# Row statistics taken in the stage before, turns interleaved with router weights, root ahead of weight copies

## Chip, cores and metric

The kernel runs on one core of a Trainium2 chip. The metric is the device time of one execution in microseconds; the median of the runs is compared. The engines are TensorE (PE), VectorE (DVE), ScalarE (ACT), GpSimd (POOL) and SyncE (SP, which only issues transfers here).

## The reference

Two transformer-like layers on x of 2048 tokens by 256 features, all float32. Each of six sublayers normalizes x first:

```python
def _layernorm(x, axis=-1, eps=1e-05):
    m = jnp.mean(x, axis=axis, keepdims=True)
    v = jnp.var(x, axis=axis, keepdims=True)
    return (x - m) / jnp.sqrt(v + eps)
...
    x = x + 0.5 * _L0_ffn_ref(_layernorm(x), ...)   # routed: 64 of 512 tokens by weight W_r, gelu FFN
    x = x + _L0_attn_ref(_layernorm(x), ...)        # latent attention, 16 heads, causal
    x = x + 0.5 * _L0_ffn_ref(_layernorm(x), ...)   # the same routed FFN
    x = x + 0.5 * _L1_ffn_ref(_layernorm(x), ...)   # sum over 8 factors, 256 x 256
    x = x + _L1_attn_ref(_layernorm(x), ...)        # attention, 16 heads of 16, rotary, causal
    x = x + 0.5 * _L1_ffn_ref(_layernorm(x), ...)
```

The change touches how mean and variance of each token are taken and when, and the order of the work that follows a normalization. Nothing else of the computation changes.

## The kernel before

x stays in SBUF all the time as 16 tiles (NT) of 128 tokens by 256 features; four tiles make a chunk (NCH = 4, CH = 512 tokens). The stages follow each other with a barrier of all engines between them (`core.end_step`): ffn_a (routed), the projections of the latent attention (latp, norm latn) and its heads (lath), ffn_b (routed), mix_a (factors), the projections of the second attention (attp, norm attn), its heads (atth), its output (atto), and mix_b, which also stores the result. Every engine has one instruction queue and works it in order; instructions wait on semaphores.

A stage with a normalization begins with `Norm.statistics` on DVE: for each of the 16 tiles `bn_stats` (L238), then for each `bn_aggr` (L241) to mean and variance, then variance + eps (L243). ACT takes the root (L259; a table load for Sqrt stands ahead of it when another function's table is in place), DVE makes 1/root with one correction step (L270 to L274). `Norm.scale` (L249) then writes the normalized tiles xn, one instruction per tile. `Turn` transposes xn: PE makes eight transposes per chunk (L204) into two PSUM banks, DVE copies one (L188), ACT the other (L193).

- **Routed stages.** `norm.vector` scales all tiles and copies all of DVE's banks before w_r_wide, the router weights spread over 128 columns, is written (L345). PE turns all four chunks, then multiplies w_r_wide with each chunk (L437); ACT copies the rows of weights (L414), PE transposes them (L443), DVE picks them up (L352) and compares all tokens with all (L358, 16 instructions, 128 x 2048 to bf16). In ffn_b SP also loads the eight factors of the mix stages; POOL waits for them and for all of xn, adds them up (L335, seven instructions) and halves the bias (L337).
- **mix stages.** Turns and products with the summed factors (L550) are already interleaved. DVE adds each result of two tiles to x (L521, eight pairs); POOL adds the bias to x (L512).
- **lath.** A planner writes the order of each engine out by hand. At its end, DVE: fold (L1320), reciprocal of the sums (L1326), scaling (L1333) and the additions to x, two tiles each (L1339), in the chunk order 0, 3, 2, 1 for each pair of heads.
- **attp.** SP loads Wq, Wk, Wv, Wo (L1579), then rotary tables and a select matrix. POOL fills v_one with ones (L1628), a single instruction of 128 x 4608. PE waits for the weights, transposes them (L1693), then runs `norm.tensor`. ACT copies the four turned weights (L1644), then select (L1646), and only then takes the root and its share of the turns. DVE runs `norm.vector`. The first projection product is L1704.
- **atto.** Turns of the attended values, products (L1985), additions of pairs to x on DVE (L1968).

Of the kernel before, what the change touches and what calls it, by code (L numbers as in the profile page):

```python
# [13 lines left out]
P = 128  # L14
# [76 lines left out]
class Core:  # L91


    def __init__(self, nc, ctx, inp):
# [6 lines left out]
        self.half_bias = self.sb("half_bias", [P, DIM], F32)  # L101
        self.ident = self.square[:, 0, :]
# [65 lines left out]
class Turn:  # L168
# [21 lines left out]
    def scalar(self, act):  # L190
        for b in range(1, 2 * NCH, 2):
            act.wait_ge(self.turned, b + 1)
            self.core.nc.scalar.activation(self.place(b), self.banks[b % len(self.banks)][:], ACT.Copy).then_inc(self.evac_act, 1)  # L193
# [19 lines left out]

class Norm:
# [5 lines left out]
    def __init__(self, core, ctx, tag, xn, xn_t, banks, loading=None):  # L220
        self.core, self.xn, self.loading = core, xn, loading
        self.stats = core.sb(f"{tag}_stats", [P, NT, 6], F32, ctx)
        self.moments = core.sb(f"{tag}_moments", [P, NT, 2], F32, ctx)
# [9 lines left out]
    def statistics(self, dve, link):  # L233
        nc, x = self.core.nc, self.core.x
        for t in range(NT):
            if self.loading and t % TPC == 0:
                dve.wait_ge(self.loading.x_loaded[t // TPC], 16)
            s = nc.vector.bn_stats(self.stats[:, t, :], x[:, t, :])  # L238
        link(s)
        for t in range(NT):  # L240
            s = nc.vector.bn_aggr(self.moments[:, t, :], self.stats[:, t, :])  # L241
        link(s)
# [8 lines left out]

    def vector(self, dve, link):
# [4 lines left out]
    def scalar(self, act):  # L257
        act.wait_ge(self.var_ready, 1)
        self.core.nc.scalar.activation(self.root[:], self.var[:], ACT.Sqrt).then_inc(self.root_ready, 1)  # L259
        self.turn.scalar(act)  # L260
# [16 lines left out]
def routed_ffn_stage(core, tag, first=False):  # L277
# [3 lines left out]
    with ExitStack() as ctx:  # L281
# [20 lines left out]
        norm = Norm(core, ctx, tag, xn, xn_t, bank, loading)  # L302
# [6 lines left out]
        with nc.Block() as block:  # L309
# [31 lines left out]
            def _(dve):  # L341
                link = Link(core, dve, f"{tag}_dve_link")
                norm.vector(dve, link)
                dve.wait_ge(s["weights_loaded"], 32)
                nc.vector.tensor_copy(w_r_wide[:], w_r[:].unsqueeze(2).broadcast_to([P, ND, P])).then_inc(s["wide_ready"], 1)  # L345
                if first:
# [3 lines left out]
                for c in range(NCH):  # L350
                    dve.wait_ge(s["weight_turned"], c + 1)
                    w = nc.vector.tensor_copy(weight[:, TPC * c:TPC * (c + 1)],  # L352
                                              bank[4 + c][:].rearrange("p (t q) -> p t q", q=P)[:, :, 0])
# [52 lines left out]
            def _(act):  # L406
                if first:
                    loading.scalar(act)
                norm.scalar(act)

                act.wait_ge(s["weights_loaded"], 32)
                for c in range(NCH):
                    act.wait_ge(s["weight_bank"], c + 1)
                    nc.scalar.activation(weight_row[:, c * CH:(c + 1) * CH], bank[c][:], ACT.Identity,  # L414
# [1606 lines left out]
```

## Time and profile before

| | us |
|---|---|
| runs of the kernel | 1922.64, 1924.5, 1932.9 (median 1924.5) |
| profiled execution, its own time | 1925.92 |
| its span in the trace | 1924.2 |
| PE busy | 1711.6 (89%) |
| DVE busy | 1513.2 (79%) |
| ACT busy | 1181.4 (61%) |
| POOL busy | 1004.6 (52%) |

The busy shares are means over stages with different limits. The long stages (lath from about 160 to 1215, atth from about 1420 to 1870) keep PE busy; the short ones between them have stretches in which a single engine works. Line numbers are those of the kernel before. A matmul in float32 is two instructions in the trace where its moving side is wide, and the trace's granted clock is 1.00 for 2.4 GHz and 0.50 for 1.2 GHz.

### The profile page before, as it was taken

To read this page: it belongs to the slowest core of one execution; us is meant where nothing else is said; L and a number is where in the kernel's file an instruction comes from. 1 tells how busy PE (TensorE), PEld (TensorE's weight loads), DVE (VectorE), ACT (ScalarE), POOL (GpSimd) and SP (SyncE) were. 2 spreads that over 40 slices of the span, in tenths; PEclk is the share of its full clock that TensorE was granted. 3 is DMA by queue.
4 is the path that set the end of the run, shared out by engine and by line. 5 is a ranking of instruction groups with operands and counts; after the bars stand their busy time and mean duration, and the time that the engine had idled before them with its cause. 6 is when DMAs were issued, how large, how long until landed. Compare 5 with 4: busy or idle time off the path is not lost. (4 is left out here: it accounts for less than half of the span.)

```text
span 1924.2 us, 27185 instructions
## 1 busy us (share of the span) xinstructions
PE 1711.6 (89%) x9368; PEld 996.5 (52%) x9368; DVE 1513.2 (79%) x2231; ACT 1181.4 (61%) x2043; POOL 1004.6 (52%) x829
## 2 busy tenths in 40 slices
PE   4667999999999999999999999566979899999986
PEld 3544555556565555565565554365644344444445
DVE  6772888998897988998879898576566988888815
ACT  1045787787776777777777776201325377778760
POOL 0004799897896997988979978202412000000111
PEclk8786999999999999999999999777977699999998
DMA  3100000000000000000000000301440200110001
GB/s 102 59 21 24 1 1 1 15 1 8 8 1 15 1 1 15 1 13 3 1 7 1 1 1 1 94 1 39 77 78 2 34 2 2 22 15 2 2 1 44
DMA packets 26697, 34.34 MB, mean 18 GB/s; under 512 B 5312, under 2 KB 19648, under 8 KB 26432
## 3 DMA queue, kind: packets, MB, share of 16 engines
q1 hardware_dynamic: 25360, 31.28, 6.8%
q8 instruction: 76, 1.25, 0.3%
q10 hardware_dynamic: 1200, 1.31, 0.2%
q14 instruction: 61, 0.50, 0.1%
HBM read 26.03 MB, written 6.29 MB: 17 GB/s over the span
## 5 line engine op out<-in xcount | busy, mean ns | idle before, releaser
L1225 POOL TENSOR_TENSOR lath_summed<-lath_summed,lath_held 128x512 f32<-128x512 f32 x392 | 525.0, 1339 | 54.4 <-ACT lath_held L1131 27.5
L1942 ACT ACTIVATE atth_probs<-atth_score 128x512 f32<-128x512 f32 (+3 forms) x640 | 293.1, 538 | 141.4 <-PE atth_score L1861 139.8
L1296 DVE TENSOR_TENSOR lath_held<-lath_held,lath_shift 128x1024 f32<-128x1024 f32 (+2 forms) x352 | 331.2, 968 | 24.6 <-PE lath_shift L1044 15.1
L1125 ACT ACTIVATE lath_held<-lath_score 128x1024 f32<-128x1024 f32 (+2 forms) x352 | 283.8, 829 | 104.9 <-DVE lath_largest L1249 51.5
L1131 ACT ACTIVATE lath_held<-lath_held 128x1024 f32<-128x1024 f32 (+2 forms) x352 | 292.6, 861 | 48.8 <-DVE lath_held L1296 47.2
L1901 DVE TENSOR_REDUCE atth_maxima<-atth_slot 128x2 f32<-128x1024 f32 (+3 forms) x288 | 287.1, 1042 | 42.2 <-PE atth_slot L1844 41.3
L1031 PE MATMUL lath_out<-lath_held,lat_latent 128*64 128x512 f32 (+1 forms) x1152 | 302.9, 590 | 8.0 <-ACT lath_held L1131 4.4
L1015 PE MATMUL lath_score<-lath_query_hi,lat_key_hi 128*128 128x512 f32 x576 | 246.7, 428 | 22.9 <-ACT lath_held L1125 17.7
L1789 POOL TENSOR_SCALAR_AFFINE_SELECT atth_probs<-atth_probs 128x512 f32<-128x512 f32 x64 | 40.7, 636 | 419.4 <-ACT atth_probs L1942 419.4
L1020 PE MATMUL lath_score<-lath_query_hi,lat_key_lo 128*128 128x512 f32 x576 | 231.1, 401 | 0.0
L1249 DVE TENSOR_TENSOR lath_largest<-lath_score,lath_largest 128x1024 f32<-128x1024 f32 (+2 forms) x240 | 211.6, 882 | 17.6 <-PE lath_score L1020 12.6
L1016 PE MATMUL lath_score<-lath_query_lo,lat_key_hi 128*128 128x512 f32 x576 | 219.6, 381 | 0.0
L1015 PEld LDWEIGHTS lath_score<-lath_query_hi,lat_key_hi 128*128 128x128 f32 x576 | 108.8, 189 | 155.0 <-issue 80.6
L1231 POOL TENSOR_TENSOR lath_turn_a<-lath_query,lat_rope 128x512 f32<-128x512 f32 x64 | 86.5, 1352 | 189.9 <-DVE lath_turn_b L1302 155.3
L1874 PE MATMUL atth_out<-atth_probs,att_v_one 128*32 128x512 f32 (+3 forms) x1280 | 151.2, 553 | 0.5 <-POOL atth_probs L1789 0.5
L1020 PEld LDWEIGHTS lath_score<-lath_query_hi,lat_key_lo 128*128 128x128 f32 x576 | 110.3, 192 | 19.9
L1016 PEld LDWEIGHTS lath_score<-lath_query_lo,lat_key_hi 128*128 128x128 f32 x576 | 109.2, 190 | 14.5
L1861 PE MATMUL atth_score<-atth_query,att_key 50*128 50x512 f32 (+3 forms) x384 | 114.3, 440 | 2.8 <-ACT atth_probs L1942 2.6
L1031 PEld LDWEIGHTS lath_out<-lath_held,lat_latent 128*64 128x64 f32 x1152 | 61.8, 135 | 92.4 <-issue 69.6
L1302 DVE TENSOR_TENSOR lath_turn_b<-lath_turn_b,lat_rope 64x512 f32<-64x512 f32 x64 | 76.6, 1198 | 31.2 <-ACT lath_turn_b L1158 29.7
L1861 PEld LDWEIGHTS atth_score<-atth_query,att_key 50*128 50x128 f32 x384 | 51.8, 186 | 90.9 <-ACT atth_probs L1942 82.9
L1241 POOL TENSOR_TENSOR lath_query_lo<-lath_query,lath_query_hi 128x512 fp32r<-128x512 f32 x64 | 83.8, 1310 | 15.1 <-ACT lath_query_hi L1165 15.1
(345 smaller groups left out, 2889.2 us busy)
## 6 DMA issues: line engine op xcount, KB each, us to landing
att_first_query<-att_scratch SPq DMA_DIRECT2D x12, 256.0 KB, 9.1
atth_query<-att_scratch SPq DMA_DIRECT2D x12, 256.0 KB, 9.8
ffn_a_w<-in_L_ffn_W SPq DMA_DIRECT2D x2, 1024.0 KB
lat_raw_out<-in_L_attn_w_out SPq DMA_DIRECT2D x8, 256.0 KB, 2.7
lat_rope<-in_c_rope_feature SPq DMA_DIRECT2D x1, 2048.0 KB, 10.3
ffn_b_w<-in_L_ffn_W SPq DMA_DIRECT2D x2, 1024.0 KB, 7.1
ffn_b_factors<-in_L_ffn_factors SPq DMA_DIRECT2D x8, 256.0 KB, 5.0
att_scratch<-attp_high SPq DMA_DIRECT2D x4, 512.0 KB, 3.2
```

Of the source, the lines that this page charges most:

```text
L1015: nc.tensor.matmul(scores, key_hi[:, keys], hi, start=True, stop=False)
L1016: nc.tensor.matmul(scores, key_hi[:, keys], lo, start=False, stop=False)
L1020: last = nc.tensor.matmul(scores, key_lo[:, keys], hi, start=False, stop=True)
L1031: last = nc.tensor.matmul(by_head(out_bank[KL * i:KL * i + KL, :], q0), latent[:, kt, 0:KL], by_head(slot(n)[:, i, :], q0), start=(step == ...
L1125: nc.scalar.activation(part_columns(slot(n), tiles, q0), part_columns(score_bank[n % 2], tiles, q0), ACT.Copy)\
L1131: nc.scalar.activation(columns, columns, ACT.Exp, scale=SCALE0)\
L1225: nc.gpsimd.tensor_tensor(total, total, slot(n)[:, i, :], ALU.add).then_inc(s["tiles_summed"], 1)
L1249: nc.vector.tensor_tensor(out, first, second, ALU.max).then_inc(s["maxed"], 1)
L1296: nc.vector.tensor_tensor(columns, columns, added, ALU.subtract)\
L1861: nc.tensor.matmul(score_bank[u % 3][:, q0:CH], key_rows(GROUP * g + h, PLACED + 2, kt * P, P), query_rows(n, h, PLACED + 2, q0, CH - q0), ...
L1901: nc.vector.reduce_max(maxima[:, n % 2, :, pair, i, at], slot[r % 2][:, :, begin:begin + width], AX.X)\
L1942: nc.scalar.activation(probs[:, step % PROB_STEPS, h, q0:CH], score_bank[u % 3][:, q0:CH], ACT.Exp, scale=SCALE1)\
```

## The change

1. A class `Measure` takes `bn_stats` of tiles as soon as x is final in them and `bn_aggr` a little later, both on DVE, in the stage that finishes x: in lath for ffn_b, in mix_a for attn, in atto for mix_b. `Norm(..., measured=True)` then skips both loops; the other three norms (ffn_a, latn, mix_a) keep them. The places for them, row_stats and row_moments, are now shared.
2. At the end of ACT's work in lath and in atto stands a Sqrt of one column.
3. In both routed stages DVE scales two chunks, writes w_r_wide, then alternates copies of turned banks with the scaling of the next chunk; PE alternates turns and router products; ACT alternates its turn copies with the copies of the weight rows. Turns use banks 0 to 3, products 4 to 7, the transposed rows 0 to 3.
4. In attp ACT takes the root first and two turn copies before the weight copies, PE turns two chunks before it waits for the weights, and DVE alternates scaling and copies.

```diff
+class Measure:
+    def count(self, tiles):
+        for t in tiles:
+            self.core.nc.vector.bn_stats(self.core.row_stats[:, t, :], self.core.x[:, t, :]).then_inc(self.counted, 1)
...
+    def gather(self, dve, tiles):
+        dve.wait_ge(self.counted, max(self.count_of[t] for t in tiles))
+        for t in tiles:
+            self.core.nc.vector.bn_aggr(self.core.row_moments[:, t, :], self.core.row_stats[:, t, :]).then_inc(self.gathered, 1)
...
     def statistics(self, dve, link):
+        if not self.measured:
...
+    def scale_and_turn(self, dve):
+        self.scale((0, 1))
+        for c in range(2, NCH):
+            self.turn.vector(dve, (c - 2,))
+            self.scale((c,))
+        self.turn.vector(dve, range(NCH - 2, NCH))
```

The routed stages, on DVE, ACT and PE:

```diff
-                norm.vector(dve, link)
+                norm.statistics(dve, link)
+                norm.scale((0, 1))
                 dve.wait_ge(s["weights_loaded"], 32)
                 nc.vector.tensor_copy(w_r_wide[:], ...).then_inc(s["wide_ready"], 1)
+                for c in range(2, NCH):
+                    norm.turn.vector(dve, (c - 2,))
+                    norm.scale((c,))
+                norm.turn.vector(dve, range(NCH - 2, NCH))
...
-                norm.scalar(act)
-
+                norm.take_root(act)
                 act.wait_ge(s["weights_loaded"], 32)
...
+                norm.turn.scalar(act, (0, 1))
+                for c in range(2, NCH):
+                    take_row(c - 2)
+                    norm.turn.scalar(act, (c,))
+                for c in range(NCH - 2, NCH):
+                    take_row(c)
...
+                norm.turn.tensor(pe, (0, 1))
+                pe.wait_ge(s["wide_ready"], 1)
+                for c in range(2, NCH):
+                    weigh(c - 2)
+                    norm.turn.tensor(pe, (c,))
+                for c in range(NCH - 2, NCH):
+                    weigh(c)
```

mix_a (atto has the same four lines after its addition, and both end with a last gather and a wait for all):

```diff
+                        if measure:
+                            dve.wait_ge(added, b + 1)
+                            measure.count((2 * b, 2 * b + 1))
+                            if b:
+                                measure.gather(dve, (2 * b - 2, 2 * b - 1))
```

lath, on DVE (`last_chunk` is the last of the 32 chunks of all head pairs), and at the end of ACT's queue:

```diff
                     if kind == "fold": ...
+                        if n == 2 * last_chunk + 1:
+                            measure.count(tiles_of(last_chunk - 1))
                     elif kind == "turn_sums_out": ...
+                        if n == last_chunk:
+                            measure.gather(dve, [t for k in range(last_chunk - 3, last_chunk) for t in tiles_of(k)])
                     elif kind == "project_out": ...
+                        if n == last_chunk - 1 and part:
+                            wait_projected(n, part)
+                            measure.count(tiles_of(n - 2) + tiles_of(n - 1))
+                        elif n == last_chunk:
+                            wait_projected(n, part)
+                            measure.count(tiles_of(n, (part,)))
+                measure.gather(dve, tiles_of(last_chunk))
+                measure.wait_all(dve)
...
+                nc.scalar.activation(core.table_scratch[:], core.ones[:, 0:1], ACT.Sqrt)
```

attp, on DVE, ACT and PE:

```diff
-                norm.vector(dve, Link(core, dve, "attp_link"))
+                norm.statistics(dve, Link(core, dve, "attp_link"))
+                norm.scale_and_turn(dve)
...
+                norm.take_root(act)
+                norm.turn.scalar(act, (0, 1))
                 for m in range(4):
                     act.wait_ge(s["weights_turned"], m + 1)
...
+                norm.turn.scalar(act, range(2, NCH))
                 act.wait_ge(s["select_loaded"], 32)
...
-                norm.scalar(act)
...
+                norm.turn.tensor(pe, (0, 1))
                 pe.wait_ge(s["weights_loaded"], 64)
...
-                norm.tensor(pe)
+                norm.turn.tensor(pe, range(2, NCH))
```

## Rows read from the trace of the kernel before

**Rows 1.** The page's first part: busy time, share of the span, instructions of each engine.

```profile
PE 1711.6 (89%) x9368; PEld 996.5 (52%) x9368; DVE 1513.2 (79%) x2231; ACT 1181.4 (61%) x2043; POOL 1004.6 (52%) x829
```

**Rows 2.** Timeline, start of ffn_b: start us, us, engine, line, operation, count, idle before.

```profile
1216.25 1.28 ACT L259 ACT_TABLE_LOAD   x1 [7.33 <-PEq L122]
1216.29 5.33 DVE L238 BATCH_NORM_STATS2 ffn_b_stats<-x 128x6 f32<-128x256 f32 x16 [0.91 <-PEq L122]
...
1222.85 0.17 DVE L243 TENSOR_SCALAR ffn_b_var<-ffn_b_moments 128x16 f32<-128x16 f32 x1
...
1224.43 5.25 DVE L249 TENSOR_SCALAR ffn_b_xn<-x,ffn_b_moments,ffn_b_rstd 128x256 f32<-128x256 f32 x16
```

**Rows 3.** Timeline, PE in the turns and router products of ffn_a, then ffn_b.

```profile
17.96 6.23 PE L204 MATMUL ffn_a_bank<-square,ffn_a_xn 128*128 128x128 f32 x32 [17.96 <-DVE ffn_a_xn L249]
...
24.73 7.13 PE L437 MATMUL ffn_a_bank<-ffn_a_xn_t,ffn_a_w_r_wide 128*128 128x512 f32 x16 [0.55 <-DVE ffn_a_w_r_wide L345]
...
1225.86 6.44 PE L204 MATMUL ffn_b_bank<-square,ffn_b_xn 128*128 128x128 f32 x32 [11.21 <-DVE ffn_b_xn L249]
```

**Rows 4.** Timeline, DVE at the end of the heads stage lath.

```profile
1204.42 0.85 DVE L1320 TENSOR_TENSOR lath_out_whole<-lath_out,lath_half 64x256 f32<-64x256 f32 x2 [3.33 <-ACT lath_half L1144]
...
1214.69 0.69 DVE L1339 TENSOR_TENSOR x<-lath_side,x 128x512 f32<-128x512 f32 x1 [0.93 <-PE lath_side L1070]
```

**Rows 5.** Timeline of ffn_b's compares, POOL beside them; by line: ns min/median/max.

```profile
1233.23 1.29 POOL L335 TENSOR_TENSOR mixed<-ffn_b_factors 128x512 f32<-128x512 f32 x1 [27.99 <-DMA ffn_b_factors<-in_L_ffn_factors]
...
1241.97 1.71 DVE L358 TENSOR_SCALAR ffn_b_not_above<-ffn_b_weight_row,ffn_b_weight 128x2048 bf16<-128x2048 f32 x1
...
1242.64 2.62 POOL L337 TENSOR_SCALAR half_bias<-half_bias 128x256 f32<-128x256 f32 x1
...
1243.60 1.41 DVE L358 TENSOR_SCALAR ffn_b_not_above<-ffn_b_weight_row,ffn_b_weight 128x2048 bf16<-128x2048 f32 x1
...
L358 DVE TENSOR_SCALAR ffn_b_not_above<-ffn_b_weight_row,ffn_b_weight x16: 1268/1273/1711, 1242.0 to 1260.6; 128x2048 bf16<-128x2048 f32 x16
...
L1302 DVE TENSOR_TENSOR lath_turn_b<-lath_turn_b,lat_rope x64: 687/1212/1829, 155.1 to 1125.0; 64x512 f32<-64x512 f32 x64
```

**Rows 6.** Timeline, end of mix_a and start of attp.

```profile
1318.17 1.28 DVE L521 SCALAR_TENSOR_TENSOR x<-mix_a_bank,x 128x512 f32<-128x512 f32 x2
...
1324.91 0.69 DVE L521 SCALAR_TENSOR_TENSOR x<-mix_a_bank,x 128x512 f32<-128x512 f32 x1 [0.96 <-PE mix_a_bank L550]
1326.56 3.94 POOL L1628 MEMSET att_v_one<- 128x4608 f32 x1 [7.33 <-POOLq L122]
1326.60 5.33 DVE L238 BATCH_NORM_STATS2 attn_stats<-x 128x6 f32<-128x256 f32 x16 [0.99 <-PEq L122]
...
1332.41 3.68 PE L1693 MATMUL attp_bank<-square,attp_raw 128*128 128x128 f32 x16 [7.54 <-DMA attp_raw<-in_L_attn_Wo]
...
1337.81 0.25 DVE L270 RECIPROCAL attn_rstd<-attn_root 128x16 f32<-128x16 f32 x1 [4.47 <-ACT attn_root L259]
...
1340.37 3.67 PE L204 MATMUL attp_bank<-square,att_attended 128*128 128x128 f32 x16 [4.28 <-DVE att_attended L249]
...
1344.93 1.94 PE L204 MATMUL attp_bank<-square,att_attended 128*128 128x128 f32 x16 [0.89 <-DVE attp_xn_t L188]
...
1346.71 1.88 PE L1704 MATMUL attp_bank<-attp_w_qkv_t,attp_xn_t 128*128 128x512 f32 x4
```

**Rows 7.** Timeline, end of atto and start of mix_b.

```profile
1889.23 0.69 DVE L1968 TENSOR_TENSOR x<-atto_bank,x 128x512 f32<-128x512 f32 x1 [1.03 <-PE atto_bank L1985]
...
1890.88 5.32 DVE L238 BATCH_NORM_STATS2 mix_b_stats<-x 128x6 f32<-128x256 f32 x16 [0.96 <-PEq L122]
...
1897.43 0.17 DVE L243 TENSOR_SCALAR mix_b_var<-mix_b_moments 128x16 f32<-128x16 f32 x1
```

**Rows 8.** Busy time by stretch in the attention heads; PEclk is the granted clock.

```profile
1440.00:1460.00 20.00, 20.00 (x103) 10.31 (x103) 9.01 (x18) 9.09 (x22) 3.18 (x5) 0.50 0.01 2
1464.00:1484.00 20.00, 19.88 (x173) 10.36 (x175) 16.28 (x25) 14.46 (x42) 5.72 (x9) 1.00 0.01 2
```

More of the change, by code:

```diff
@@ L188, in vector, with scalar @@
             self.core.nc.vector.tensor_copy(self.place(b), self.banks[b % len(self.banks)][:]).then_inc(self.evac_dve, 1)
-    def scalar(self, act):
-        for b in range(1, 2 * NCH, 2):
+    def scalar(self, act, chunks=range(NCH)):
+        for b in (ND * c + 1 for c in chunks):
             act.wait_ge(self.turned, b + 1)
@@ L234, in statistics @@
         nc, x = self.core.nc, self.core.x
[L235 to L242, printed above, removed]
+        if not self.measured:
+            for t in range(NT):
+                if self.loading and t % TPC == 0:
+                    dve.wait_ge(self.loading.x_loaded[t // TPC], 16)
+                s = nc.vector.bn_stats(self.stats[:, t, :], x[:, t, :])
+            link(s)
+            for t in range(NT):
+                s = nc.vector.bn_aggr(self.moments[:, t, :], self.stats[:, t, :])
+            link(s)
         nc.vector.tensor_scalar(self.var[:], self.moments[:, :, 1], LN_EPS, None, ALU.add).then_inc(self.var_ready, 1)
@@ L301, in routed_ffn_stage @@
         loading = Loading(core, ctx) if first else None
-        norm = Norm(core, ctx, tag, xn, xn_t, bank, loading)
+        norm = Norm(core, ctx, tag, xn, xn_t, bank[:4], loading, measured=not first)
         names = ("weights_loaded ffn_loaded wide_ready weight_bank row_ready weight_turned compared counted chosen_ready"
@@ L431, in _, with weigh @@
             def _(pe):
-                norm.tensor(pe)
-                pe.wait_ge(s["wide_ready"], 1)
-                for c in range(NCH):
+                def weigh(c):
                     norm.turn.wait_chunk(pe, c)
                     for k in range(ND):
-                        last = nc.tensor.matmul(bank[c][:], w_r_wide[:, k, :], xn_t[:, k, c * CH:(c + 1) * CH],
+                        last = nc.tensor.matmul(bank[4 + c][:], w_r_wide[:, k, :], xn_t[:, k, c * CH:(c + 1) * CH],
                                                 start=(k == 0), stop=(k == ND - 1))
                     last.then_inc(s["weight_bank"], 1)
+                if first:
+                    pe.wait_ge(loading.square_loaded, 16)
+                norm.turn.tensor(pe, (0, 1))
[5 more added lines that the diff above has]
+                    weigh(c)
                 for c in range(NCH):
@@ L442, in _ @@
                     for i in range(TPC):
-                        last = nc.tensor.transpose(bank[4 + c][:, i * P:(i + 1) * P],
+                        last = nc.tensor.transpose(bank[c][:, i * P:(i + 1) * P],
                                                    weight_row[:, c * CH + i * P:c * CH + (i + 1) * P], core.ident)
@@ L503, in mixed_ffn_stage @@
         bank = [ctx.enter_context(nc.psum_tensor(f"{tag}_bank{i}", [P, CH], F32)) for i in range(8)]
-        norm = Norm(core, ctx, tag, xn, xn_t, bank[:4])
+        norm = Norm(core, ctx, tag, xn, xn_t, bank[:4], measured=out is not None)
+        measure = Measure(core, tag) if out is None else None
         mixed_done, added, biased, stored = (core.sem(f"{tag}_{n}") for n in ("mixed_done", "added", "biased", "stored"))
@@ L963, in latent_heads @@
         side_free = [core.sem(f"lath_side_free{i}") for i in range(2)]
+        measure = Measure(core, "lath")
+        last_chunk = NCH * PAIRS - 1
         def side(event):
@@ L1255, in _, with tiles_of, wait_projected @@
                 dve.wait_ge(s["vector_constants"], 1)
+                def tiles_of(k, parts=range(2)):
+                    return [TPC * LATENT_CHUNKS[k % NCH] + 2 * part + i for part in parts for i in range(2)]
+                def wait_projected(k, part):
+                    dve.wait_ge(freed(("project", k, part)), use["project", k, part] // 2 + 1)
                 for kind, n, *a in plan["vector"]:
@@ L1960, in attention_output @@
         projected, added = core.sem("atto_projected"), core.sem("atto_added")
+        measure = Measure(core, "atto")
         with nc.Block() as block:
@@ L1973, in _ @@
                 turn.scalar(act)
+                nc.scalar.activation(core.table_scratch[:], core.ones[:, 0:1], ACT.Sqrt)
             @block.tensor
```

42 lines of the change are left out of this document (31 added, 11 removed).

## The prediction

> **What bounds the kernel now.** I read the busy shares first [rows 1]: TensorE (PE) is busy for 89% of the span, VectorE (DVE) for 79%, so over the whole kernel the change can matter only where PE stands idle. Then the timeline at each stage start. There the picture is the same in ffn_b, attn and mix_b: all engines met at a barrier, PE has nothing to do, and one chain on DVE runs alone: 16 statistics of 256 columns (5.33 us), 16 aggregates (1.2 until the variance), variance, root, reciprocal, then the scaling of which PE needs four tiles before its first turn. In ffn_b the first DVE instruction is at 1216.29, the variance at 1222.85, scaling at 1224.43, PE at 1225.86 [rows 2, 3]. These microseconds are on the path one for one. The prices I use: 0.33 us per statistic and 0.07 per aggregate back to back (5.33/16, 1.2/16), and about 0.04 for a wait on an own semaphore. Third come the ends of the stages before, where the statistics go: what is idle there on DVE [rows 4, 6, 7].
>
> **The change part by part**, S being DVE's first instruction of a stage in the trace, S' the same after the change.
>
> *ffn_b, statistics out.* The variance comes at S instead of S + 6.56 (1222.85 - 1216.29): **-6.56**. The table load of 1.28 that hid behind the statistics [rows 2] moves to the end of the heads stage, where ScalarE (ACT) is idle; cost 0, and 1.1 if it stayed.
>
> *Heads stage, statistics in.* Twelve of sixteen tiles are counted in DVE's gaps: eight (2.7 us) after the last but one chunk's addition, ahead of an instruction before which DVE idled 3.33, four (1.4) and twelve aggregates (0.9) in later gaps [rows 4]; 0, for nobody is queued behind them on DVE before those gaps end. Of the last chunk two tiles fit into the 0.93 idle before the last addition (needed: 0.04 + 0.74). What follows that addition is bare: wait 0.04, two statistics 0.74, wait, four aggregates 0.4: **+1.2**.
>
> *Turns interleaved with router weights (ffn_a and ffn_b).* Before, PE ran 32 transposes (6.23 and 6.44), waited 0.55 for w_r_wide, then 7.13 of router products [rows 3]: 13.9 from first to last. The transposes took about 0.2 each, twice the 0.11 of the fast stretch of attn [rows 6], so this was TensorE at 1.2 GHz. After, PE has the same work without the wait: 32 x 0.11 + 6.9 = 10.4 us at 2.4 GHz, plus half of the time until the clock rises. If it rises 5 to 5.6 us after PE starts, as the pace of [rows 3] says, that is 12.9 to 13.2, a gain of 0.7 to 1.0; if after 3.7, as in attn [rows 6], 1.6. DVE keeps up: two chunks 2.6, wide copy 0.3, copy 0.7, then 1.3 per chunk. ACT's row copies stand behind turns in one queue, but each waits for products that PE issues earlier. **-1.0 each, -2.0.** DVE now waits for the weights at about S' + 4.3 with the scaling of chunks 2 and 3 queued behind, and PE behind that. The trace has no such wait; in attn a megabyte had landed 5.8 after the stage's start [rows 6], and here the two loads are tiny and issued first: 0, at most 1.5.
>
> *What the earlier compares meet.* The 16 compares of ffn_b come about 8 us earlier against GpSimd (POOL), whose seven additions of factors wait for a DMA and don't move (S + 17, [rows 5]). Before, only the last addition and the half_bias scaling overlapped them: the first compare took 1.71 instead of 1.27, the next 1.41, so DVE lost 0.44 + 0.14 + 0.14 = 0.7. After, compares begin near S' + 18 with some five or six additions left. Cheapest, as half_bias: twice 0.14 each, 1.6 in all. Dearest, as the slowest DVE product beside POOL in the heads (1829 against 687, 1.14 each [rows 5]): 6 x 1.14 = 6.8 more. Below nothing too: if compares kept POOL out altogether, -0.7. An addition reads twice half_bias's columns from two inputs, so I take a middle price of 0.7 each: **+3.5**, ends -0.7 and +7.
>
> The Trainium skill, "SBUF — State Buffer", section "Who interferes with whom", says that a VectorE instruction in a two-port mode (tensor_scalar from SBUF to SBUF can be one) and a GpSimd instruction lock each other out for the whole instruction. By that rule the first compare's 0.44 is right, but half_bias, 2.62 long while two compares each lost only 0.14, is not plainly so. It speaks against this change in two places; what it gives is rival B.
>
> *mix_a, statistics in.* After each pair's addition DVE now waits (0.04), counts two tiles (0.66) and aggregates two older ones (0.14): 0.69 + 0.84 = 1.53 per pair, against the 1.65 in which PE delivers one (0.69 and 0.96 idle, [rows 6]). But DVE starts late: the first two pairs fit ahead of the copy that precedes 1318.17; from there six pairs come back to back, 1318.2 + 6 x 1.53 = 1327.4, and a last wait with aggregates 0.3. Before it ended at 1325.60. **+2.1** (bounds 1.1, the bare tail alone, to 2.5). PE isn't held: it needs the addition four pairs back.
>
> *attn.* Before: DVE's variance was ready early, but the root stood behind the weight copies in ACT's queue (DVE idle 4.47), PE turned at S + 13.8, and the first projection product came at 1346.71, S + 20.1 [rows 6]. After: root at once, scaling possible at S' + 1.6. There POOL's memset of v_one runs until S' + 3.9. Statistics ran beside it undisturbed (5.33, as in ffn_b), but the scaling is of the compares' kind, which POOL delayed [rows 5]; no row shows one beside a memset. Bounds: 0 and 2.3; I take 2.3 as the compare is the nearer row. Then scaling at S' + 3.9, PE 1.43 later at 5.35 with 48 transposes (16 turns, 16 weight turns whose data landed at 5.8, 16 turns): 3.7 us at 1.2 GHz do 17 of them, 31 x 0.11 the rest, so the product at about **S' + 12.6**: **-7.5**. Without the memset's delay it would be about 10.2. The ACT queue moves too: two turn copies, four weight copies, two turn copies, select; select is first needed only after the first products, and the DMA that it waits for is issued as before: 0.
>
> *atto and mix_b.* Pairs of atto come every 1.72 (0.69 and 1.03 idle), so 1.53 fits; after the last addition (1889.92) wait, two statistics, aggregates: **+1.1**. The variance of mix_b comes 6.55 earlier (1897.43 - 1890.88): **-6.55** [rows 7]. The table load moves as in ffn_b. What follows is the unchanged PE chain.
>
> Sum: -6.56 + 1.2 - 2.0 + 3.5 + 2.1 - 7.5 + 1.1 - 6.55 = **-14.7**. The profiled execution took 1925.92 (span 1924.2), 1.4 above the median of the runs, 1924.5. So 1911.2 for such a run and **1910** for the median.
>
> **Where it could go otherwise.**
>
> *A, POOL costs nothing.* For: statistics ran undisturbed beside the memset; half_bias cost little. Against: the 1.71 compare and the 1212 median of the heads' products [rows 5]. Then -3.5 and -2.4: **1904**.
>
> *B, whole-instruction exclusion.* Each POOL addition in turn holds back a compare (+3.5 over my term), and the memset, issued 0.04 before DVE starts, holds even the tiny variance: scaling at S' + 5.5 and the first product at S' + 14.1 (+1.5). For: the 1.14. Against: 0.14. **1915**.
>
> *C, the change doesn't do what it says with the table.* If the table load stays in front of the root of ffn_b and mix_b, each gets 1.1 back: **1912**. Against: attn has no load before its root, since mix_a's table was still in place.
>
> *D, slower.* The attention heads begin with a dense PE stretch at 1.2 GHz: from 1440 to 1460 PE is busy all 20.00 us at a granted 0.50 with 103 matmuls, from 1464 to 1484 there are 173 at 1.00 [rows 8]. Nothing in the work tells the two apart. If after the shift the clock rose later, each microsecond so spent costs 0.4 (1 - 103/173). From 37 us more the gain of 14.7 is eaten; 60 more give **1934**. For: the run at 1932.9. Against: the other two runs and the profile agree within 3.5 us. It may also rise earlier, to 9 us faster.
>
> **How the numbers follow.** Forecast 0.48, A 0.22, B 0.20, C 0.06, D 0.04. The forecast's own range comes from the clock's rise at four stage starts (0.8 each) and the tails: 1907 to 1913. A downwards with the clock in luck gives 1902, B upwards 1917; that leaves out D and the edges, so 1902 to 1917. Faster by over 0.5% (about what a measurement of this kernel can tell from no change) is below 1914.9: all of A, nearly all of the forecast and C, half of B: 0.80. Within 0.5%: half of B, part of the rest: 0.17. Slower: what D holds beyond 1934: 0.03.
>
> **What would show it.** In the changed kernel's profile: (1) ffn_b's scaling 1.6 after DVE's first instruction and PE 3.0 after; (2) about 0.9 + 1.2 between the heads' last addition and that first instruction; (3) compares of ffn_b starting at S' + 18 instead of S + 25.7, and lasting 19.9 (1260.6 + 1.27 - 1242.0, [rows 5]) plus the POOL term; (4) mix_a's last addition about 1 later relative to its stage, attn's first DVE instruction 2.1 later; (5) attn's first scaling at S' + 1.6, 3.9 or 5.5, which tells A, forecast and B apart, and the first product at S' + 12.6; (6) mix_b's PE 3.0 after its start; (7) no table load at the starts of ffn_b and mix_b; (8) the granted clock of the heads between 1430 and 1480. The prediction is wrong if additions on POOL cost the compares over 7 us, if a gap in the heads' tail is too short so that folds or reciprocals start late, or if the clock of the attention heads behaves otherwise.

## The result and the profile after

| | before | after |
|---|---|---|
| median of the runs (14 each) | 1925.22 us | 1915.11 us |
| lowest and highest | 1922.31, 1940.16 | 1912.81, 1925.87 |
| profiled execution, its span | 1925.92, 1924.2 | 1915.44, 1913.7 |

The ratio of after to before is 0.9942, with a 95% interval of 0.992 to 0.9964: some 0.6% faster. The predicted time was 1910, the range 1902 to 1917. The forecast sum was -14.7 us; the two profiled spans differ by 10.5.

The page's first part of the changed kernel, in the form of [rows 1]:

```profile
PE 1710.8 (89%) x9368; PEld 995.6 (52%) x9368; DVE 1523.4 (80%) x2231; ACT 1181.7 (62%) x2045; POOL 1010.2 (53%) x829
```

PE does the same work. DVE is busy 10.2 us more and POOL 5.6 more, although neither has more instructions. That growth is the first sign of what went wrong in the sum: instructions that stretch.

In what follows S' is the start of DVE's first instruction in a stage of the changed kernel, as in the prediction.

Start of ffn_b after, with the end of the heads stage ahead of it (timeline of DVE; start, us, engine, line, operation, count, idle before), to be held against [rows 2] and [rows 4]:

```profile
1201.81 2.71 DVE L226 BATCH_NORM_STATS2 row_stats<-x 128x6 f32<-128x256 f32 x8
...
1215.38 0.69 DVE L1419 TENSOR_TENSOR x<-lath_side,x 128x512 f32<-128x512 f32 x1 [0.22 <-PE lath_side L1138]
1216.10 0.75 DVE L226 BATCH_NORM_STATS2 row_stats<-x 128x6 f32<-128x256 f32 x2
1216.89 0.38 DVE L233 BATCH_NORM_AGGREGATE row_moments<-row_stats 128x2 f32<-128x6 f32 x4
1218.42 0.17 DVE L270 TENSOR_SCALAR ffn_b_var<-row_moments 128x16 f32<-128x16 f32 x1 [1.15 <-PEq L124]
...
1220.00 2.67 DVE L276 TENSOR_SCALAR ffn_b_xn<-x,row_moments,ffn_b_rstd 128x256 f32<-128x256 f32 x8
```

The variance is DVE's first instruction of the stage, and the scaling comes 1.58 after the start of that instruction; before, it came 8.14 after the start of the stage's first. The bare tail is two statistics and four aggregates. Mix_b looks the same (variance 1885.97, scaling 1887.56).

The compares of ffn_b after, with the POOL instructions that now run among them (timeline; then the group by line with ns min/median/max), against [rows 5]:

```profile
1235.21 1.26 POOL L372 TENSOR_TENSOR mixed<-ffn_b_factors 128x512 f32<-128x512 f32 x1 [29.28 <-DMA ffn_b_factors<-in_L_ffn_factors]
1235.94 25.89 DVE L400 TENSOR_SCALAR ffn_b_not_above<-ffn_b_weight_row,ffn_b_weight 128x2048 bf16<-128x2048 f32 x16
1236.56 13.16 POOL L372 TENSOR_TENSOR mixed<-mixed,ffn_b_factors 128x512 f32<-128x512 f32 x6
1242.03 0.59 PE L510 MATMUL ffn_b_bank<-masks,ffn_b_not_above 128*128 128x1 bf16 x16 [1.62 <-DVE ffn_b_not_above L400]
1244.24 0.59 PE L510 MATMUL ffn_b_bank<-masks,ffn_b_not_above 128*128 128x1 bf16 x16 [1.62 <-DVE ffn_b_not_above L400]
1249.77 2.61 POOL L374 TENSOR_SCALAR half_bias<-half_bias 128x256 f32<-128x256 f32 x1
...
L400 DVE TENSOR_SCALAR ffn_b_not_above<-ffn_b_weight_row,ffn_b_weight x16: 1270/1408/2286, 1235.9 to 1260.6; 128x2048 bf16<-128x2048 f32 x16
```

The whole group takes 25.89 (19.91 before). PE counts each compare as it ends, so PE's rows are a clock for them: 1242.03, 1244.24, one every 2.20, while the six additions take 13.16, also 2.19 each. Compare and addition alternate. Each of the first seven compares ends 1.08 after an addition does, and a compare alone takes 1.28: so it had worked beside the last 0.2 of that addition at most, and had waited before that.

Start of attp after (timeline), against [rows 6]:

```profile
1326.50 3.94 POOL L1717 MEMSET att_v_one<- 128x4608 f32 x1 [8.56 <-POOLq L124]
1326.54 3.92 DVE L270 TENSOR_SCALAR attn_var<-row_moments 128x16 f32<-128x16 f32 x1 [1.03 <-PEq L124]
1331.88 2.67 DVE L276 TENSOR_SCALAR att_attended<-x,row_moments,attn_rstd 128x256 f32<-128x256 f32 x8
1333.31 3.67 PE L206 MATMUL attp_bank<-square,att_attended 128*128 128x128 f32 x16 [10.40 <-DVE att_attended L276]
1340.91 1.88 PE L1796 MATMUL attp_bank<-attp_w_qkv_t,attp_xn_t 128*128 128x512 f32 x4
```

The variance covers 16 columns and takes 3.92, ending 0.02 after the memset. The same instruction takes 0.17 in ffn_b. Scaling is at S' + 5.34, the first projection product at S' + 14.37.

The terms side by side, each from one mark to the next in the two profiled executions (us):

| term | forecast | measured | from, to |
|---|---|---|---|
| ffn_b, statistics out | -6.56 | -6.56 | first DVE instruction to scaling 8.14, 1.58 |
| heads stage, tail | +1.2 | +1.44 | last addition to ffn_b's first DVE instruction 1.60, 3.04 |
| interleaving, both stages | -2.0 | -1.96 | scaling to first compare: 17.42, 17.06 and 17.54, 15.94 |
| compares of ffn_b | +3.5 | +5.98 | first to end of last 19.91, 25.89 |
| mix_a, tail | +2.1 | +1.91 | DVE's last turn copy to its first instruction of attp 9.03, 10.94 |
| attn | -7.5 | -5.74 | first DVE instruction to first projection product 20.11, 14.37 |
| atto, tail | +1.1 | +1.08 | last addition to mix_b's first DVE instruction 1.65, 2.73 |
| mix_b, statistics out | -6.55 | -6.55 | first DVE instruction to scaling 8.14, 1.59 |
| sum | -14.7 | -10.4 | span difference -10.5 |

Of the 4.3 us that are missing, 2.5 lie in the compares and 1.8 in attn, both places where POOL runs beside DVE.

That the sum comes so near the span difference is partly luck. The stretches between these marks, to which the prediction gave nothing, moved too and cancel: about 1.1 longer ahead of the end of the heads stage, 1.2 shorter from ffn_b's compares to mix_a's variance, 0.7 shorter from there to mix_a's last turn copy, and 1.0 longer in mix_b behind its scaling. The last is no scatter of one profile: PE starts 1.44 after the scaling in both kernels, but its first 16 products take 3.63 before and 4.61 after (granted clock in the 4 us from just behind their start 1.00 and 0.76), and in every profile of a kernel that takes mix_b's statistics in atto the stretch is longer than before, by 0.1 in one and 0.7 to 1.2 in the others. So of the 6.55 by which the scaling of mix_b moved, some 1.0 was lost again to the slower clock behind it.

### The profile page after: what moved, and what is told of

It is laid out like the page before. It is cut to its first block and busy times, and to the rows that moved or that the text cites. A ratio compares the mean times of both kernels' runs of the same rounds, so it can differ in the third digit from the quotient of the medians.

```text
span 1913.7 us, 27197 instructions
## 1 busy us (share of the span) xinstructions
PE 1710.8 (89%) x9368; PEld 995.6 (52%) x9368; DVE 1523.4 (80%) x2231; ACT 1181.7 (62%) x2045; POOL 1010.2 (53%) x829
## 5 line engine op out<-in xcount | busy, mean ns | idle before, releaser
L1318 DVE TENSOR_TENSOR lath_largest<-lath_score,lath_largest 128x1024 f32<-128x1024 f32 (+2 forms) x240 | 211.7, 882 | 17.5 <-PE lath_score L1088 12.5
L1084 PEld LDWEIGHTS lath_score<-lath_query_lo,lat_key_hi 128*128 128x128 f32 x576 | 109.3, 190 | 14.7
## 6 DMA issues: line engine op xcount, KB each, us to landing
lat_rope<-in_c_rope_feature SPq DMA_DIRECT2D x1, 2048.0 KB, 10.5
```

The costliest lines, as they stand in the source:

```text
L1084: nc.tensor.matmul(scores, key_hi[:, keys], lo, start=False, stop=False)
L1318: nc.vector.tensor_tensor(out, first, second, ALU.max).then_inc(s["maxed"], 1)
```

## The experiments

**Two theories.** *Exclusion* (rival B): a DVE tensor_scalar with its operands in SBUF and a POOL instruction never run together; each waits until the other's whole instruction is over, and a tiny one waits as long as a large one. *Clock or chance*: the compares and attn were slow because TensorE's clock or a late transfer happened to fall badly in this execution, and POOL is a bystander. The first two kernels move only the POOL work and leave every instruction in.

**memset_late.** The memset of v_one waits until the scaling is done; one line is added ahead of it:

```
+                pool.wait_ge(norm.xn_ready, NT)
```

> The changed kernel, with GpSimd's memset of v_one held back until all scaled tiles of attn are written. Theory (the memset keeps VectorE's variance, a tensor_scalar from SBUF to SBUF, from starting: it took 3.92 us beside the memset and 0.17 elsewhere): the variance takes 0.17 again, scaling starts 1.6 us after the stage's first VectorE instruction instead of 5.3, and the first projection product comes about 3.5 us earlier; time about 1911.5. Rival (VectorE's variance waited for something else, as the barrier or the moments of the stage before): it stays at 3.9 and the time at 1915.

Timeline of memset_late at the start of attp:

```profile
1325.76 0.17 DVE L270 TENSOR_SCALAR attn_var<-row_moments 128x16 f32<-128x16 f32 x1 [1.03 <-PEq L124]
1327.33 2.67 DVE L276 TENSOR_SCALAR att_attended<-x,row_moments,attn_rstd 128x256 f32<-128x256 f32 x8
1333.85 3.94 POOL L1718 MEMSET att_v_one<- 128x4608 f32 x1 [16.71 <-DVE att_attended L276]
1336.54 1.88 PE L1797 MATMUL attp_bank<-attp_w_qkv_t,attp_xn_t 128*128 128x512 f32 x4
```

The variance is back at 0.17, scaling at S' + 1.57, the product at S' + 10.78 instead of 14.37: 3.6 us gained in the stage. The whole run took 1914.52 and not the expected 1911.5, since the attention heads behind it took 440.5 us where they took 437.4 in the profile of after; a section below is on that. The mechanism is confirmed at its place and the expectation of the total was wrong.

**adds_late.** The factor additions and half_bias of ffn_b wait for the copies of one-hot rows, beyond the compares:

```
-                    pool.wait_ge(norm.xn_ready, NT)
+                    pool.wait_ge(s["onehot_t_dve"], 2)
```

> The changed kernel, with GpSimd's additions of the factors in ffn_b held back until the transposed one-hot tiles are copied (they then run beside VectorE instructions that read PSUM). Theory (each addition keeps one compare waiting): all 16 compares take 1.27 to 1.29 us, from the first to the end of the last 19.2 us instead of 26, so about 6 us less in the stage and a time of about 1909. Rival (the compares are slow because TensorE's counts at 1.2 GHz hold them back): the additions change nothing there, 1915. A further rival: the additions now delay mix_a or the end of ffn_b and give 2 to 6 us back.

Adds_late: the compares by line (ns), and POOL's timeline:

```profile
L400 DVE TENSOR_SCALAR ffn_b_not_above<-ffn_b_weight_row,ffn_b_weight x16: 1281/1282/1286, 1235.7 to 1253.6; 128x2048 bf16<-128x2048 f32 x16
...
1272.80 8.01 POOL L372 TENSOR_TENSOR mixed<-mixed,ffn_b_factors 128x512 f32<-128x512 f32 x6
1280.87 0.85 POOL L374 TENSOR_SCALAR half_bias<-half_bias 128x256 f32<-128x256 f32 x1
```

All 16 compares take 1.28, the group 19.22 instead of 25.89 (-6.7), half_bias 0.85 instead of 2.61, and the six additions 8.01 instead of 13.16. DVE is idle there for part of the time (5.85 us) and then reads PSUM in instructions of 0.42 and 0.43 each, as long as in after. Nothing in the stage waits for the later additions: from the last compare to mix_a's variance it takes 39.9 us, where it took 40.0. The run took 1908.28, and its heads 437.3, as in after's profile: the total moved by 7.2, of which 6.7 is this.

**both_late.** Both edits together, run six times.

> The changed kernel with both: memset and factor additions moved out from under VectorE's two-port work. If the two costs are separate places of one chain, they add: about 9.5 us below the changed kernel, 1905 to 1906, a ratio to the kernel before of 0.9895. If one hides behind the other or behind the clock, less than 7.

The median of six runs is 1907.01 (1905.08 to 1911.7), the ratio to the kernel before 0.9892, interval 0.9861 to 0.9924. Compares 19.22, product at S' + 10.75: both gains stand side by side, and outside the attention heads this profile is 11.3 us shorter than that of after. By the medians the kernel is 8.1 us below after, by the lowest runs (1922.25 before, 1912.81 after, 1905.08 here) 7.7; 9.5 was expected and the two places give 10.3. The six runs don't say where the rest went; in the one profile the heads took 443.7 against 437.4. All six runs lie below the lowest of after, though the two were not run side by side. So it beats the kernel before beyond doubt, and the changed kernel as far as these runs can tell.

**no_interleave.** The routed stages keep the old order, all turns and then all router products:

```
-                norm.turn.tensor(pe, (0, 1))
-                for c in range(2, NCH):
-                    weigh(c - 2)
-                    norm.turn.tensor(pe, (c,))
+                norm.turn.tensor(pe)
+                for c in range(NCH):
+                    weigh(c)
```

> The changed kernel with the old order in the routed stages (all scaling and copies, then the wide router weights, then all turns, then all products; banks as before). My step said 1.0 us for each of the two stages. Expected: from scaling to the first compare 17.4 to 17.5 us again in both stages, against 17.1 in ffn_a and 15.9 in ffn_b with the interleaving; time 1 to 3 us above 1915. In ffn_b the compares begin 1.6 us later, so one addition of GpSimd fewer is in their way and up to 1.3 of it comes back: then the total is near 1915.

From scaling to the first compare it took 17.73 in ffn_a, a little more than expected, and 17.02 in ffn_b, a little less. Among the profiles of kernels with the interleaved order ffn_a ranges from 15.58 to 17.06 and ffn_b from 15.40 to 16.70. The samples of the old order, here and in before (17.42, 17.54), all lie above those, so interleaving gains, between 0.3 and 2 us a stage and about 1 in the middle; a closer figure these runs don't give. Part of it is lost again in ffn_b: without the interleaving the compares start later and meet less of the additions, and take 25.18 where the two profiles of the changed kernel have 25.89 and 26.56. The run's 1925.08 tells little of it: its heads took 443.9.

**after_again.** The changed kernel itself, a second profile.

> The changed kernel itself, unchanged, for a second profile. In the profiles so far the attention heads (from their first shift_t to atto's first turn copy) took 437.2 to 437.4 us in three kernels, 440.5 in one and 443.8 in two, although none of the edits touches them; TensorE's clock fell earlier or rose later in the longer ones. Theory (the clock's moments differ from execution to execution): every part outside the heads as in the first profile within 1.5 us, the heads one of these lengths or another. Rival (each kernel's shift fixes where the clock moves): the heads take 437.4 again and the total is within 0.5 of 1913.7 in span.

Span 1920.7 instead of 1913.7, with the same instructions. Attn's scaling is at S' + 5.33 again and the compares are long again (26.56, 25.89 in after), while other marks move: ffn_a's first compare 15.58 behind its scaling instead of 17.06, heads 440.6 instead of 437.4. Outside the heads the whole is 3.8 longer, and 2.0 of that lie in one part, the projections of the latent attention, so the expected 1.5 did not hold. A single run's total can't judge an edit of 3 us here, and the marks inside a stage can. For the record, the runs of the five kernels below took 1920.44 (var_two_inputs), 1920.48 (no_early_table), 1918.46 (attn_stats_home), 1922.79 (attn_order_before) and 1904.85 (attn_stats_home_late), with heads of 444.0, 440.2, 437.2, 438.5 and 433.3.

**var_two_inputs.** The memset stays early; the variance becomes a two-input addition of a tile that holds epsilon:

```
-        nc.vector.tensor_scalar(self.var[:], self.moments[:, :, 1], LN_EPS, None, ALU.add)
+        nc.vector.tensor_tensor(self.var[:], self.moments[:, :, 1], self.core.eps[:], ALU.add)
```

> The changed kernel, with each norm's variance + eps as a tensor_tensor of moments and a tile of eps (filled once in ffn_a) instead of a tensor_scalar; the memset of v_one stays where it was. Theory (the memset keeps out only VectorE instructions that use both of its port pairs, as tensor_scalar from SBUF to SBUF does; one with two SBUF inputs isn't held by work that only writes): attn's variance takes 0.2 us beside the memset, the root, the reciprocal and two products follow at once, and the next tensor_scalar of the correction step is what waits until the memset ends, 3.9 after the stage's start; scaling at about 4.2 instead of 5.3, total about 1 us less. Rival (the memset holds any small VectorE instruction that writes SBUF): variance 3.9 again, scaling at 5.3.

Timeline of var_two_inputs at the start of attp:

```profile
1324.96 3.94 POOL L1721 MEMSET att_v_one<- 128x4608 f32 x1 [8.48 <-POOLq L125]
1325.00 0.17 DVE L274 TENSOR_TENSOR attn_var<-row_moments,eps 128x16 f32<-128x16 f32 x1 [1.03 <-PEq L125]
...
1325.95 0.17 DVE L313 TENSOR_TENSOR attn_scratch<-attn_scratch,attn_var 128x16 f32<-128x16 f32 x1
1326.16 2.77 DVE L314 TENSOR_SCALAR attn_scratch<-attn_scratch 128x16 f32<-128x16 f32 x1
1329.17 2.67 DVE L280 TENSOR_SCALAR att_attended<-x,row_moments,attn_rstd 128x256 f32<-128x256 f32 x8
```

This is the sharpest of the runs. Beside the memset the two-input additions and products take their usual 0.17; the first tensor_scalar in the chain, the correction, takes 2.77 and ends 0.03 after the memset does. Scaling is at S' + 4.17 instead of 5.34, as expected, while the expected microsecond in the total drowned in heads of 444.0. Which instruction the memset holds goes by its form, whatever its place or size. A late transfer or a clock can't choose so.

That two inputs go free holds for the memset, which reads nothing. POOL's instructions in the heads stage of lath have two inputs in SBUF, and they do hold such products. In the trace of after (by line; ns min/median/max):

```profile
L1378 DVE TENSOR_TENSOR lath_turn_b<-lath_turn_b,lat_rope x64: 687/1196/1787, 155.2 to 1125.7; 64x512 f32<-64x512 f32 x64
```

Of these 64 products 55 are issued while a POOL instruction runs, and 48 of them end 0.55 after that instruction does. A product alone takes 0.69, so they too had worked beside its last 0.14 at most.

**no_early_table.** The two one-column square roots that fetch the table ahead of time are left out:

> The changed kernel without the two Sqrt instructions of one column at the end of ScalarE's work in lath and atto. The table load of 1.28 us should then stand at the start of ffn_b and of mix_b, with the variance waiting for it: from the variance to the scaling 2.7 instead of 1.6 us in both stages, 2.2 us in all (my rival C). If the load is placed earlier by itself, nothing.

Timeline of no_early_table at the start of ffn_b:

```profile
1217.15 1.28 ACT L293 ACT_TABLE_LOAD   x1 [8.85 <-PEq L124]
1217.19 0.17 DVE L270 TENSOR_SCALAR ffn_b_var<-row_moments 128x16 f32<-128x16 f32 x1 [1.15 <-PEq L124]
1218.44 0.22 ACT L293 ACTIVATE ffn_b_root<-ffn_b_var 128x16 f32<-128x16 f32 x1
...
1219.82 2.67 DVE L276 TENSOR_SCALAR ffn_b_xn<-x,row_moments,ffn_b_rstd 128x256 f32<-128x256 f32 x8
```

The load stands in front of the root again: scaling 2.63 after the start of the variance instead of 1.58, in mix_b too. Each of the two early loads is worth 1.05.

**attn_stats_home, attn_order_before, attn_stats_home_late.** The change did two things to attn: statistics moved into mix_a, and the root went ahead of the weight copies. These undo one at a time. In attn_stats_home attn takes its own statistics and keeps the new order (its norm also loses `measured=True`):

```
-        measure = Measure(core, tag) if out is None else None
+        measure = None
```

> The changed kernel, but attn takes its own statistics again (mix_a measures nothing); root ahead of the weight copies and interleaved turns stay, and so does the memset at the stage's start. The statistics run under the memset, so the variance comes 6.6 after the stage's start and scaling at 8.1 instead of 5.3; mix_a ends 1.9 earlier. If that is all, moving these statistics gained only about 0.9 us and the root's place and the interleaving gained the rest of attn's 5.8. If the move itself was the gain, the first projection product comes 3 us or more later than in the changed kernel.

In attn_order_before the statistics stay in mix_a and ACT and PE keep the old order (weight copies, then root):

```
-                norm.take_root(act)
-                norm.turn.scalar(act, (0, 1))
...
+                norm.scalar(act)
```

> The changed kernel, but in attn the order of before (weight turns, weight copies and select ahead of the root, scaling of all tiles ahead of all copies), with the statistics still taken in mix_a. Theory (the gain of attn is the root's place; the moved statistics were off the path there): the root waits for the select copy as before, the first projection product comes 20.1 us after the stage's first VectorE instruction as before, so 5.7 later than in the changed kernel, and the move of the statistics by itself costs mix_a's 1.9 and gives nothing. Rival (the statistics were on attn's path): the product comes 3 us or more before 20.1.

Attn_stats_home_late is attn_stats_home with both edits of both_late:

> The kernel with memset and factor additions late, but attn takes its own statistics and mix_a none. With the memset out of the way the moved statistics should be worth their length less mix_a's tail: scaling 8.1 after the stage's start against 1.6, mix_a 1.9 earlier, so the first projection product about 4.6 us later than in the kernel with both late, measured from the last copy of turns in mix_a; with the memset in front (the run before) it was 1.2 to 1.5. If the product comes less than 2.5 later, the memset was not what hid the gain.

Since the tail in mix_a belongs to the price, the mark is from mix_a's last turn copy to attn's first projection product (us):

| statistics | root | memset early | memset late |
|---|---|---|---|
| in attn | after weight copies | 29.14 (before) | |
| in mix_a | after weight copies | 31.46 | |
| in attn | first | 26.12 | 25.73 |
| in mix_a | first | 25.31 (after) | 21.69 (both_late) |

The deciding lines are attn's variance and first product in the timeline, first of attn_stats_home:

```profile
1326.92 3.94 POOL L1717 MEMSET att_v_one<- 128x4608 f32 x1 [7.36 <-POOLq L124]
1326.96 5.33 DVE L265 BATCH_NORM_STATS2 row_stats<-x 128x6 f32<-128x256 f32 x16 [0.99 <-PEq L124]
1333.52 0.17 DVE L270 TENSOR_SCALAR attn_var<-row_moments 128x16 f32<-128x16 f32 x1
1344.05 1.88 PE L1796 MATMUL attp_bank<-attp_w_qkv_t,attp_xn_t 128*128 128x512 f32 x4
```

and of attn_order_before:

```profile
1326.00 3.92 DVE L270 TENSOR_SCALAR attn_var<-row_moments 128x16 f32<-128x16 f32 x1 [1.03 <-PEq L124]
1338.73 5.25 DVE L276 TENSOR_SCALAR att_attended<-x,row_moments,attn_rstd 128x256 f32<-128x256 f32 x16
1346.52 1.88 PE L1792 MATMUL attp_bank<-attp_w_qkv_t,attp_xn_t 128*128 128x512 f32 x4
```

The mark scatters: in the five profiles that share the attn of after it is 25.28 to 25.68, in the two with both moved and a late memset 21.69 and 21.72. In attn_order_before the product comes 20.52 behind the stage's first DVE instruction, where 20.1 was expected and is in before.

The statistics are of no hurry where the root stands behind the weight copies: moving them alone costs 2.3 (31.46 against 29.14), its tail with nothing in return. The new order alone gives 3.0 (26.12 against 29.14). Moving the statistics on top of it gives 0.4 to 0.8, because the memset, which ran free beside the statistics, then holds the variance. With the memset out of the way the same move gives 4.0 (21.69 against 25.73). So most of attn's gain in the change as made comes from the order, and of the 7.45 (29.14 - 21.69) that order and statistics give with a late memset it got 3.83. The expected worth of the statistics there was 4.6. The 0.6 went to the turns behind: the 16 transposes of weights take 2.68 in both_late and 2.07 in attn_stats_home_late, and the rest of the way from scaling to product is alike. The run of attn_stats_home_late took 1904.85 in all, less than both_late's median: its heads took 433.3, the shortest seen, so that is no verdict for its edit.

## Why the prediction was right or wrong

**Right, in part by its width.** The measured 1915.11 lies inside 1902 to 1917, but not because the forecast of 1910 held: it missed by 5, half of the gain that was measured, and the upper end of the range stood there for rival B. What follows are the terms one by one.

**Right, by the row.** Up to the scaling, the statistics of ffn_b and mix_b left the path at full price (-6.56, -6.55; in mix_b the products behind gave 1.0 back), and the tails cost what their instructions cost (+1.44, +1.91, +1.08 against +1.2, +2.1, +1.1). The heads' tail is 0.2 dearer since the barrier behind it took 1.15 and not 0.91. In mix_a the last six pairs come 1.51 apart, 1.53 forecast. Interleaving came out at -1.96 in the two profiles, -2.0 forecast, but as 0.36 in ffn_a and 1.60 in ffn_b instead of 1.0 each; the spread of the samples (1.5 us from one profile to the next) makes that hit partly luck. The router's weights, for which DVE now waits, were there in time. The table load is at 1209.55 in the heads stage, at the end, so rival C did not occur; its price of 1.1 is 1.05.

**Wrong: what the earlier compares meet.** The forecast of the place was right (compares start at S' + 17.5, six additions left), the price per addition was mis-sized: the step that failed is the middle price. I took 0.7, between half_bias's 0.14 and the heads' 1.14, and the weight of the two rows was wrong. The measured price is a compare spacing of 2.20 instead of 1.19, 1.0 each: 6 x 1.0 for the additions, 0.4 for the first compare and 0.3 for half_bias make 6.7, less the 0.7 that stood in before, +6.0. The 0.14 was real too. Half_bias takes 0.85 alone (adds_late), so even in full exclusion it could cost compares little, and most of its 2.61 among them is its own waiting: a long row with a small price, from which nothing followed for a two-input addition of 1.34. That two compares lose only 0.28 together to it, and not something nearer 0.5, these runs leave open. Rival B's +7 misses by 1.0 where my term misses by 2.5. It was too high by a slip as well: taken with six additions, +3.5 is 6 x 0.7 less the 0.7 that stood in before, and the dear end didn't take that 0.7 off; 6 x 1.14 less 0.7 is +6.1, all but the measured +5.98.

The Trainium skill, "SBUF — State Buffer", section "Who interferes with whom", calls the shared ports of VectorE and GpSimd an exclusive lock that is held for the whole instruction. The trace agrees but for the ends: compares come 1.19 apart alone, additions 1.34 (8.01/6), which makes 2.53 one behind the other; measured are 2.20, so some 0.33 overlap. With no hold at all the compares would have stayed at 1.19 and the additions at 1.34.

**Wrong: attn.** The step that failed is that only the scaling would be held, from S' + 1.6 to S' + 3.9. I asked which instructions are of the compares' kind and stopped at the scaling, though the variance in front of it is of that kind too, and is issued 0.04 after the memset. So the whole chain of 1.6 starts after the memset instead of running beneath it: scaling at S' + 5.34 where rival B gave 5.5 and the forecast 3.9. That is 1.44 of the 1.8 missing; the other 0.3 is between scaling and product. The bounds (0 and 2.3 for the hold) were too narrow, since they were bounds on the scaling's wait alone; the true wait was 3.75 at another instruction.

**The rivals.** A (POOL costs nothing) is refuted by adds_late and memset_late. B had the mechanism and the time: 1915 against a median of 1915.11, and got 0.20 where the forecast got 0.48. Its evidence for was the row of DVE products 512 columns wide beside POOL, its evidence against a single short instruction; the first should have weighed more, for the longest of those products were held by whole additions. D (the clock in the attention heads) is real as a spread of both signs, 10.7 us between the shortest and the longest heads, though no slowdown from it remains in the medians.

**What was not asked.** The prediction took moving attn's statistics and moving its root as one edit. Apart they are +2.3 and -3.0, together -3.8, and the order in which they are made decides what each seems to be worth: behind the moved statistics the new order gives 6.2, ahead of them 3.0.

## What to carry to other kernels

When work is taken off the front of a chain, list what every other engine does in the time into which the chain moves, and for POOL look at each DVE instruction by its form, tiny ones too: here a scalar operation from SBUF to SBUF waited for all but the last 0.2 us of POOL's additions and of its memset (only the short half_bias cost less), and an operation with two inputs in SBUF waited so for POOL instructions that read, though not for one that only wrote. POOL work with no one waiting for it belongs under stretches in which DVE reads PSUM; here two such waits gave back 3.6 and 6.7 us at their places. And where the clock makes single totals scatter by more than an edit is worth, measure from mark to mark inside the stage.

## What the hardware showed unexpectedly

The attention heads, from the first shifted row to atto's first turn copy, are the same instructions in all the profiles, and took from 433.3 to 444.0 us: 437.4 in after, 440.6 in the second profile of it, 440.5 in memset_late, 443.7 in both_late, 433.3 in attn_stats_home_late. The experiments ran on three chips, and the lengths differ on each of them (437.3 to 443.9 on the first, 437.2 to 444.0 on the second, 433.3 and 438.5 on the third), so the chip doesn't decide them. Busy time by stretch at the same places of the heads, 50 and 82 us behind the first shifted row, of after and then of memset_late (us, PE with count, PEld, DVE, ACT, POOL, granted clock, share and rate of DMA):

```profile
1478.10:1486.10 8.00, 5.28 (x44) 2.35 (x36) 7.80 (x10) 0.63 (x2) 0.63 (x1) 0.92 0.01 2
1510.10:1518.10 8.00, 8.00 (x40) 3.38 (x37) 6.40 (x6) 6.12 (x12) 0.00 (x0) 0.66 1.09 124
```

```profile
1473.70:1481.70 8.00, 6.03 (x42) 2.86 (x34) 6.65 (x9) 0.70 (x2) 0.64 (x1) 0.72 0.01 2
1505.70:1513.70 8.00, 7.90 (x30) 4.31 (x31) 5.98 (x7) 4.67 (x10) 0.00 (x0) 0.50 1.01 127
```

In memset_late the clock had been lowered (0.72 instead of 0.92 granted) at the first place and was still at 1.2 GHz (0.50) at the second, where in after it had risen for part of the stretch: 30 matmuls against 40 in 8 us of nearly full PE. Between 46 and 96 us behind the first shifted row memset_late falls back by 3.0 us, which is nearly all of its 3.1. What sets the moment of the fall and of the rise is open: the same program shows both courses, and no run here was made to steer it.

The second surprise is how small an instruction can be and still be held: 16 columns, 0.17 us of work, waited 3.75 us behind a 4608-column memset, while 16 statistics of 256 columns, which read one tile each, ran beside the same memset in 5.33, as they do without it.
